# Probability transposes moved behind the next step's first projection, and the second group of head transposes written into the scores' bank

## The reference

```
q, qx = LN_head(fp8lin(ln_out, wq)), LN_head(fp8lin(ln_out, wqx))      # 16 heads of 128
k, v  = LN_head(fp8lin(ln_out, wk)), fp8lin(ln_out, wv)                # 8 groups of 128
kx, vx = split(cond @ w_kv_x.T);  kx = LN_head(kx)
core = softmax(q k^T / sqrt(128)) v        # within a batch of 64 tokens, 2 heads share a group
xout = softmax(qx kx^T / sqrt(128)) vx
x = x + tanh(g0) * (fp8(clip(cat(core, xout) / smooth)) @ wproj.T) * scales
x = x + tanh(g1) * (top-2 of 16 experts, gated by a router, + one shared expert)(layernorm(x))
```

## Time and profile before

| what | value |
|---|---|
| runs | 525.98, 520.98, 527.20 us |
| profiled execution | 521.2 us, span 519.4 us |
| TensorE busy | 429.8 us, 83% of the span |
| VectorE busy | 374.1 us, 72% |
| ScalarE busy | 287.9 us, 55% |
| GpSimd busy | 233.5 us, 45% |
| attention steps | from about 24 us to 414 us of the span |
| one tile of four steps, in the middle | 42.65 us |

### The profile page before, as it was taken

How to read it: one execution, slowest core, us unless ns; L and a number is a source line. 1 busy time by engine, 2 the same in 40 slices (tenths; PEclk the granted TensorE clock), 3 DMA queues, 4 the chain that set the end, 5 groups by cost and what they waited for, 6 DMA issues and landing times.

```text
span 519.4 us, 9936 instructions
## 1 busy us (share of the span) xinstructions
PE 429.8 (83%) x2982; PEld 311.9 (60%) x2982; DVE 374.1 (72%) x846; ACT 287.9 (55%) x610; POOL 233.5 (45%) x387
## 2 busy tenths in 40 slices
PE   0587746989999999999999999999988689999930
PEld 0455525666666666666666666666667477788720
DVE  5977652698888889889888888988777853233245
ACT  3587842666756766676666766577764032323320
POOL 1253250543564365354555446443542173166660
PEclk9888985999999999999999999999999879999985
DMA  8910099999800000000000000000057033343307
GB/s 211 304 73 1 1 129 254 279 315 270 227 0 0 0 0 0 0 0 0 0 0 0 0 0 0 0 0 1 3 214 333 1 107 98 87 123 116 106 20 242
DMA packets 34811, 45.66 MB, mean 88 GB/s; under 512 B 3035, under 2 KB 32224, under 8 KB 33889
## 3 DMA queue, kind: packets, MB, share of 16 engines
q1 hardware_dynamic: 26656, 35.61, 22.5%
q0 software_dynamic: 6992, 9.46, 8.3%
q10 hardware_dynamic: 1136, 0.27, 0.3%
HBM read 28.34 MB, written 24.32 MB: 101 GB/s over the span
## 4 chain that ended last, share of the span: by engine, by line
PE 53%; issue 11%; ACT 10%; POOL 10%; DVE 8%; DMA 7%; SPq 1%; ACTq 1%; POOLq 0%; DVEq 0%
PE proj_ps L847 11%; PE score_ps L870 9%; PE headT_ps L861 6%; PE proj_ps L1000 5%; PE pv_ps L892 5%; PE proj_ps L839 5%; PE out_ps L902 4%; POOL rot L519 4%; ACT qT L669 4%; DMA wp_sb<-in_wpT 3%; ACT kT L669 2%; POOL reg L525 1%; PE pv_ps L803 1%; DMA arena<-zbuf 1%; DVE arena L1176 1%
## 5 line engine op out<-in xcount | busy, mean ns | idle before, releaser
L847 PE MATMUL proj_ps<-arena 128*128 128x512 f16 x384 | 102.1, 390 | 11.1 <-DMA wp_sb<-in_wpT 10.7
L1216 DVE BATCH_NORM_STATS2 st<-rot 128x6 f32<-128x256 f32 x192 | 72.8, 420 | 47.4 <-ACT rot L635 46.1
L635 ACT ACTIVATE rot<-proj_ps 128x512 f32<-128x512 f32 x96 | 56.7, 590 | 57.0 <-PE proj_ps L847 53.2
L861 PE MATMUL headT_ps<-idf,rot 128*128 128x128 f32 x384 | 59.5, 277 | 22.2 <-ACT qT L669 15.3
L519 POOL TENSOR_TENSOR rot<-rot,cw 128x512 f32<-128x512 f32 x64 | 70.6, 1124 | 2.5
L861 PEld LDWEIGHTS headT_ps<-idf,rot 128*128 128x128 f32 x384 | 43.3, 140 | 46.8 <-issue 33.2
L870 PEld LDWEIGHTS score_ps<-kT,qT 128*128 128x128 f32 x512 | 62.6, 196 | 7.8 <-ACT qT L669 5.3
L525 POOL TENSOR_TENSOR reg<-reg,rinv 128x512 f32<-128x512 f32 x32 | 33.4, 1045 | 73.2 <-DVE rinv L1236 73.2
L870 PE MATMUL score_ps<-kT,qT 128*128 128x64 f32 x512 | 63.2, 278 | 0.1
L847 PEld LDWEIGHTS proj_ps<-arena 128*128 (+1 forms) x384 | 37.9, 104 | 37.4 <-issue 14.7
L669 ACT ACTIVATE qT<-headT_ps,colv 128x512 f32<-128x512 f32 x64 | 49.7, 777 | 12.5 <-PE headT_ps L861 10.9
(11 more groups left out here) (215 smaller groups left out, 749.8 us busy)
## 6 DMA issues: line engine op xcount, KB each, us to landing
zbuf<-fill SPq DMA_DIRECT2D x1, 16576.5 KB, 61.8
arena<-in_wffn SPq DMA_DIRECT2D x4, 1536.0 KB, 13.5
arena<-zbuf SPq DMA_DIRECT2D x32, 128.5 KB, 2.1
wkv_stage<-in_wkvN SPq DMA_DIRECT2D x1, 2048.0 KB, 14.9
wp_sb<-in_wpT POOLq DMA_DIRECT2D x1, 2048.0 KB, 15.6
wp_sb<-ybuf SPq DMA_DIRECT2D x8, 256.0 KB, 4.9
xs<-in_x SPq DMA_DIRECT2D x2, 512.0 KB, 5.0
wp_sb<-in_wqN POOLq DMA_DIRECT2D x1, 1024.0 KB, 12.4
```

Source lines behind the costliest of these rows:

```text
L635: act.activation(raw[c % 2][i], proj_ps[i % 2][:, :], ACT.Copy).then_inc(proj_evac, 1)
L847: mm = pe.matmul(ps, lhs, w[kind][:, ch, 512 * b:512 * b + 512], start=(k == 0), stop=(k == 3))
L861: mm = pe.transpose(dst, raw[c % 2][i][:, h * D:(h + 1) * D], idf[:, :])
L1216: ins = ve.bn_stats(st[:, 4 * i + h:4 * i + h + 2, :].rearrange("p h s -> p (h s)"), raw[c % 2][i][:, h * D:(h + 2) * D].rearrange("p (h d ...
```

## The change

TensorE transposes the probabilities of n-3 after the first projection of step n, where it transposed those of n-2 near the end. ScalarE's copy of them moves likewise, from between `heads_out` 1 and 2 to behind the evacuation of bank 0. The second group of head transposes (i == 1) writes `score_ps` and waits for `sub_done`; the third group still writes `headT_ps` and now waits only for the copy of the first.

```diff
@@ scalar: heads_out
-                act.activation(dst, headT_ps[:, :].rearrange("p (h t) -> p h t", h=4), ACT.Identity,
+                ps = (headT_ps, score_ps, headT_ps)[i]
+                act.activation(dst, ps[:, :].rearrange("p (h t) -> p h t", h=4), ACT.Identity,
                                scale=col(kind + "w"), bias=col(kind + "b")).then_inc(headT_evac, 1)
@@ scalar: step
                     evacuate(n, c, 0)
                 for j in next_folds(n, 0):
                     fold_high(j)
+                if live(n, 3):
+                    prob_copy(n - 3, (c - 3) % 2)
                 if heads:
                     norm_bank0(n - 1, before)
...
                     heads_out(n - 1, before, 1)
-                if attend:
-                    prob_copy(n - 2, c % 2)
                 if heads:
                     heads_out(n - 1, before, 2)
@@ tensor: head_transposes
                 pe.wait_ge((norm0_done, norm1_done, norm2_done)[i], n + 1)
-                ge(pe, headT_evac, 3 * n + i)
+                if i == 1:
+                    ge(pe, sub_done, n)
+                else:
+                    ge(pe, headT_evac, 3 * n + (0, 0, 1)[i])
+                ps = (headT_ps, score_ps, headT_ps)[i]
                 for h in range(4):
                     if i > 0:
-                        dst = headT_ps[:, :].rearrange("p (g b h s) -> p g b h s", g=2, b=2, h=2)\
+                        dst = ps[:, :].rearrange("p (g b h s) -> p g b h s", g=2, b=2, h=2)\
                             [:, h // 2, :, h % 2, :]
                     else:
-                        dst = headT_ps[:, h * P:(h + 1) * P]
+                        dst = ps[:, h * P:(h + 1) * P]
@@ tensor: step
                 for j in next_folds(n, 0):
                     fold(j)
+                if live(n, 3):
+                    prob_transposes(n - 3, (c - 3) % 2)
                 if attend:
                     scores(n - 2, c % 2)
...
                     head_transposes(n - 1, before, 1)
-                if attend:
-                    prob_transposes(n - 2, c % 2)
                 if heads:
                     head_transposes(n - 1, before, 2)
```

## The result

The changed kernel takes 504.49 us (median of four runs, 503.88 to 505.16) against 523.48 us before (520.48 to 527.20): a ratio of 0.963, 95% interval 0.956 to 0.971. The forecast was 499 us in a range of 491 to 511. Its profiled execution took 503.9 us with a span of 502.0, against 521.2 and 519.4 before. In this and the later groups, runs more than 1.5% above the fastest of their kernel are left out of the ratios. The direction was right and the size somewhat too large: the span lost 17.4 us, where the working had 23.3.

The account below looks back on a forecast made before the run. TensorE, then ScalarE, bounds three steps, VectorE c = 2. Terms 17.0 + 3.6 + 3.0 - 0.9 + 0.6 = 23.3 us off 521.2 gave 497.9; a quarter of the gap to the median made 499 (491 to 511).

Parts of the forecast that it names:

- rival A: The forecast itself: the step-by-step walk holds, 491 to 503 us; chance 0.70.
- rival B: VectorE becomes the bound and meets GpSimd more often; a tile saves 1.6 us, 506 us in all; chance 0.17.
- Steps c = 0, 1 and 3: Three of a tile's four steps: shorter by 0.84, 1.05 and 0.88 us.
- step c = 2: VectorE's step: expo stays at 284.16; steps c = 1 and 2 together save 1.12 us.
- The two waits on one bank, and the copy's slot: End of step: waits of 0.29 + 0.59 us on one bank go, and heads_out 2 takes the copy's place.
- The copy's new place: Ahead of the four scalings, covered by their 1.28 us wait: priced at nothing, otherwise 0 to 0.6 us a step.
- The half clock: Step 1: the moved transposes run with a copy at half clock, costing 0.9 us (0.4 to 1.2).
- first steps: Steps 1 and 2: the load of the output weights lands earlier, 3.0 us saved (0.9 to 3.5).
- the tail: Steps 33 and 34: 0.6 us gained (-1 to 1), the last values product covered by 3.3 us.
- Steps 28 to 31: Steps without DMA or folds: 0.9 us each, 3.6 us saved (2 to 4.5).
- The second group's wait for sub_done: Head transposes 1 wait for the subtraction instead of heads_out 0; in c = 2 nearly a tie, priced at nothing.
- rival D: Slower: head transposes 1 behind sub_done, every step then lasts 11.40 us, about 545 us; chance 0.04.

Follow-up runs that it names:

- part-alone kernels: Only the bank change, 529.61 us, and only the move of transposes and copy, 533.02 us, each against the kernel before at 524.75 us.
- the second trace: The changed kernel run again, unaltered, as the base of a later group: 504.45 us, ratio 0.969 to the kernel before.

## Why the prediction was right, and where it was too large

**The total.** 504.5 us lies in the range. It is 1.5 us above the bounds of rival A, the forecast (491 to 503), and 1.5 below the price of rival B (506). Steps c = 0, 1 and 3 went as A had it; step c = 2 went as neither, by B's mechanism, VectorE's meetings with GpSimd.

**The two waits on one bank, and the copy's slot.** Right. c = 0 was forecast 0.84 us shorter and is 0.93; c = 1 1.05 and 1.06; c = 3 0.88 and 0.98. The walk put ScalarE last in c = 0 and TensorE last in the other two. In the trace of after TensorE has at most 0.02 us of idle left in any of them. In c = 0 heads_out 1 starts 0.59 us after values_out where it was 0.71 before, which the walk had not counted, and that is about the 0.09 us it was off by. The part-alone kernels show that the saving needs both halves.

**The copy's new place costs nothing.** Right: in step c = 2 the four scalings still wait 1.18 us for the coefficients behind the copy, and 27 of the 32 steps show such a wait, as in the kernel before.

**Step c = 2.** Wrong in size, and the largest miss. The step named was "expo follows at 284.16 whatever TensorE does", with the meeting of VectorE and GpSimd taken as "the same single meeting as now". The chain is 0.84 us longer: two meetings of 0.72 us each in place of one of 0.59. The prediction had the shift itself right ("about 0.9 us earlier": GpSimd's scaling starts 5.28 us after the third statistics where it started at 6.21), but it did not walk on to see that the scaling now starts under the third of the five rounding operations and meets that one and the fourth. c = 1 and 2 together saved 0.32 us and not 1.12; with the 0.19 us that c = 0 and 3 gave above the forecast, six tiles saved 3.7 us less. The other end of that term, 1.2 us a tile, was in the range. Rival B had the mechanism but the wrong place: it was priced on the steps with slack, where nothing was lost, and the loss fell where there was none. The sign it was to be known by, two long rows of the subtraction L1197 in a tile, did not come either: the long rows are those of the two operations before it.

The Trainium skill's page "SBUF — State Buffer" ("SBUF: two separate sides") says that the operation that comes second waits until the first one's whole instruction has ended, and that this holds for a VectorE operation in a two-port mode as well as for one with two inputs. The rows of L1196 agree: this one-input operation ends at 309.63, so its own 0.43 us began at 309.20, which is 1.06 after GpSimd's first scaling started, and one undisturbed scaling takes 1.04. Whether L1196 runs in such a mode, no row shows. The prediction took the 0.59 us of a row that had met only the rest of an instruction as the price of a meeting.

**The half clock** was in the prediction only for the first steps. It cost 1.7 us in the middle and some of the tail: there TensorE fell to 1.2 GHz during steps 33 and 34, the shared matmuls of step 34 took 3.15 us where they had taken 1.89, and the last values product moved to within 1.6 us of its reader where 4.4 were before. The tail lost 0.3 us in this trace instead of gaining 0.6; in the second trace it gained 0.3. The cover held all the same.

**First steps.** The load of the output weights ended TensorE's wait at 78.12 us in place of 81.83, 3.7 us earlier where 3.0 was forecast. The moved transposes then took 0.85 us ahead of the scores, as forecast (0.9), so the scores of step 4 came 2.9 us earlier where the two terms gave 2.1. In part that is chance: in the second trace the load ended the wait only at 79.61. Step 4 itself got 1.45 us shorter, 0.5 more than the other steps c = 0. **Steps 28 to 31** gave 2.8 against 3.6, 0.2 of it in step 30.

Sum: 23.3, less 3.7 (six tiles of 2.22 in place of 2.84), 1.7 (half clock), 0.8 (steps 28 to 31), 0.9 (tail) and 0.1 (rounding), plus 0.8 (first steps) and 0.5 (step 4), is 17.4 us, what the span lost.

**The second group's wait for sub_done** was called a tie. It became an idle of 0.70 us in c = 2, in the place that rival D named, but the third group waited for heads_out 0 until 315.73 anyway. Giving the groups their own banks moved only 0.4 us.

## What to carry to other kernels

Where two in-order engines pass work to and fro, cost a change by a walk of both lists to the next common point, and take the halves of a change together: here one half alone saved 0.5 us a tile, the other cost 1.0, and both together saved 2.2. Compare them in a stretch at one granted clock, because the totals (each half alone 1% slower) had the clock in them. When a change shifts one engine's work against another's, look for the rows whose duration varies with what runs beside them, and price a meeting at up to the whole instruction of the other engine, first on the step whose engine has no slack. An idle engine in front of the bound one (here ScalarE, 4.1 us) is the place to put the work that disturbs it.

## What the runs showed of the hardware that was not expected

- A one-input VectorE operation of 0.43 us took 1.15 us beside GpSimd's scaling of 128 by 512 fp32, and a two-input one of 0.69 us took 1.41.
- The meeting costs GpSimd as well: its 128 by 12 operation of L508, which takes 0.21 us in 13 steps of the kernel before, took 0.65 at 306.33 in the changed one, beside a two-input VectorE operation that kept its 0.69.
- TensorE's clock fell to 1.2 GHz for 3.4 us after 4.10 us with 2.20 us of work in it, whose longest idle was 1.19 us. The same idle in the other five tiles left it at 2.4 GHz (312.11 to 316.21: 4.10 us with 2.21 of work, granted clock 1.00 there and after it). Both traces of the changed kernel had it in step 22. What decides it stays open here.
